# Windowed attention and top-1 experts on one core: the masks move from queries to keys

## What is computed

```python
q = (x @ wq.T + bq).reshape(B, S, H, D)
k = (x @ wk.T + bk).reshape(B, S, H, D)
v = (x @ wv.T + bv).reshape(B, S, H, D)
...
loc = jnp.einsum('bnihd,bnjhd->bnihj', qw, kw) * scale
...
attn = jax.nn.softmax(scores, axis=-1)
out = jnp.einsum('bihj,bjhd->bihd', attn, v).reshape(B, S, HID)
return out @ wo.T + bo
```

## Time and profile before

| | |
|---|---|
| time, median of 3 runs | 444.32 us (442.57 to 446.08) |
| profiled execution | span 442.8 us; no other time of its own is shown |
| instructions | 14658 |
| busy | PE 92%, PEld 77%, DVE 74%, ACT 57%, POOL 50% |
| attention steps | from 37.6 us (scores of window 1) to 312 us (last transposes of attn) |

### The profile page before, as it was taken

One profiled execution on the slowest core, in us unless ns is written; L12 is line 12 of the kernel. 1 busy time (PEld: TensorE's weight loads), 2 busy tenths in 40 slices (PEclk: granted clock), 3 DMA queues, 4 the chain that ended last, 5 costly groups with the idle time before them and its releaser, 6 DMA issues.

```text
span 442.8 us, 14658 instructions
## 1 busy us (share of the span) xinstructions
PE 405.3 (92%) x5747; PEld 339.8 (77%) x5747; DVE 326.1 (74%) x796; ACT 250.6 (57%) x523; POOL 220.4 (50%) x301
## 2 busy tenths in 40 slices
PE   5899799999999999999999899988798998999991
PEld 4758678888888888888888778756577887777891
DVE  6785687758757757757759888563668998899785
ACT  3424665675575575575576576676663555544421
POOL 4361343464464464464464566435733485477540
PEclk9999999999999999999999999999989999999997
DMA  8663740000000000000020000000000011011004
GB/s 240 186 199 111 240 137 4 27 25 0 24 24 0 24 24 0 24 24 0 24 72 4 25 2 3 3 1 2 0 2 2 1 49 47 0 47 49 34 15 143
DMA packets 21720, 20.34 MB, mean 46 GB/s; under 512 B 3133, under 2 KB 21682, under 8 KB 21682
## 3 DMA queue, kind: packets, MB, share of 16 engines
q1 hardware_dynamic: 16900, 15.07, 10.9%
q10 hardware_dynamic: 4782, 4.75, 3.3%
HBM read 15.41 MB, written 4.41 MB: 45 GB/s over the span
## 4 chain that ended last, share of the span: by engine, by line
PE 52%; DVE 26%; ACT 9%; issue 8%; DMA 3%; ACTq 1%; DVEq 0%; POOL 0%; POOLq 0%
DVE row_max_t L1154 10%; PE ps L1461 7%; PE ps L1737 7%; PE ps L1424 7%; PE ps L1562 5%; PE ps L1384 5%; PE ps L1415 4%; PE ps L1438 3%; PE ps L1444 3%; ACT probs L847 3%; DVE k_part L1013 2%; ACT boundsT_t L858 2%; PE ps L1406 2%; DMA rows<-in_L_attn_x_dram 2%; ACT k_part L713 2%
## 5 line engine op out<-in xcount | busy, mean ns | idle before, releaser
L847 ACT ACTIVATE probs<-ps 128x1024 f32<-128x1024 f32 x64 | 62.1, 1022 | 68.2 <-PE ps L1428 68.2
L1154 DVE TENSOR_REDUCE row_max_t<-ps 128x16 f32<-128x2048 f32 x31 | 70.9, 2287 | 3.7 <-PE ps L1415 3.6
L1737 PE MATMUL ps<-w_part,hm_part 128*128 128x256 f32 x384 | 53.8, 289 | 1.8 <-DVE hm_part L1332 1.8
L1415 PE MATMUL ps<-k_part,q_part 32*128 32x128 f32 x1584 | 51.5, 274 | 3.1 <-issue 1.5
L1415 PEld LDWEIGHTS ps<-k_part,q_part 32*128 32x128 f32 x1584 | 46.9, 186 | 9.2 <-issue 7.0
L1562 PE MATMUL ps<-xh_parts,w_part 128*128 128x512 f32 x192 | 53.8, 416 | 0.0
L557 POOL TENSOR_TENSOR q_part<-qf,q_part 128x512 fp32r<-128x512 f32 x32 | 41.0, 1281 | 25.7 <-ACT q_part L695 25.7
L599 POOL TENSOR_TENSOR attn_t<-num_t,rden_t 128x256 f32<-128x256 f32 x32 | 20.0, 624 | 64.7 <-DVE rden_t L1185 64.7
L1737 PEld LDWEIGHTS ps<-w_part,hm_part 128*128 128x128 f32 x384 | 48.2, 190 | 4.8 <-DVE hm_part L1332 2.4
L788 ACT ACTIVATE ffn_rows<-ps,b1s 128x512 f32<-128x512 f32 x32 | 22.0, 687 | 42.2 <-PE ps L1562 34.1
L1562 PEld LDWEIGHTS ps<-xh_parts,w_part 128*128 128x128 f32 x192 | 34.7, 194 | 6.5 <-issue 0.6
(11 more groups left out here) (234 smaller groups left out, 906.4 us busy)
## 6 DMA issues: line engine op xcount, KB each, us to landing
table<-rest_sums SPq DMA_DIRECT2D x4, 1088.0 KB, 6.1
xs<-in_L_attn_x_dram SPq DMA_DIRECT2D x16, 256.0 KB, 2.8
rows<-in_L_attn_x_dram ACTq DMA_DIRECT2D x4, 1024.0 KB, 8.1
out_dram<-yout SPq DMA_DIRECT2D x6, 512.0 KB, 2.9
w<-in_L_ffn_W_dram SPq DMA_DIRECT2D x2, 256.0 KB, 7.6
w<-in_L_ffn_W_dram SPq DMA_DIRECT2D x1, 512.0 KB, 4.2
out_dram<-yout SPq DMA_DIRECT2D x2, 256.0 KB, 2.6
out_dram<-yout ACTq DMA_DIRECT2D x2, 256.0 KB, 2.8
```

What stands on the lines that cost most here:

```text
L847: act.activation(probs[:, 2 * h:2 * h + 2, :], ps[:, 2 * h:2 * h + 2, :], ACT.Exp).then_inc(probs_ready, 1)
L1154: dve.tensor_reduce(row_max[:], ps_all, op=ALU.max, axis=AX.X).then_inc(max_ready, 1)
L1415: last = mm(ps[:, u, (2 * c + a) * P:(2 * c + a + 1) * P], q_part[x][quad(u), s, c, a, :], k_part[y][quad(u), s, c, :], start=(i == 0), st ...
L1737: mm(y, hm_part[a][:, 1 - p, f, c * P:(c + 1) * P], w2_part[b][:, f, :], start=(f == 0 and i == 0), stop=False)
```

## The change

1. The mask and the scale move to the key for the scores: `k_masked` holds, for the two windows of a pair, each key twice (one or the other half), in two parts. The query is kept whole (`q_whole`, high and low part). `scores` multiplies the whole query (stationary) with both masked keys (256 columns): 24 matmuls in place of 48. The turned scores keep masked queries and whole keys.
2. Who masks: the keys DVE (`mask_keys`, four instructions of 512 elements in odd steps, between the reciprocal and the residual), the queries' high part ACT (two of 512 in odd steps, ahead of the exponentials), the queries' low part POOL (one of 512 in each step, where `q_low` stood). ACT makes the whole query's high part in even steps ahead of the exponentials, DVE its low part with two instructions in place of four.
3. Odd steps: DVE's maximum comes first, the keys' low part behind the bounds and guards; on PE the first window's value product goes from ahead of the turned scores to behind the bounds' transpose, and the output product from behind the turned sums to ahead of the turned scores.
4. `k_masked` shares memory with the first expert rows' parts; so their high part is taken in step 31 and no longer in step 30. `w1` shares memory with `ysum` and is loaded at step 24 in place of the start; `split_first_layer` begins a step later.
5. The first pair's keys are masked by ACT (high) and POOL (low) ahead of the steps.

The core of the diff:

```diff
+        k_masked = [xh_parts[:, 0, i].rearrange("p c n -> p (c n)").rearrange("p (w c a n) -> p w c a n", w=2, c=KC, a=2)
+                    for i in range(2)]
...
-        qf = sb("qf", [P, 2, KC, 2, P])
+        q_whole = [sb(f"q_whole{i}", [P, SLOTS, KC, P], fp32r) for i in range(2)]
...
-            def q_low(w, s):
-                need(pool, turned_scores_in_psum, w - 3)
-                pool.wait_ge(q_high_ready, w // 2 + 1)
-                pool.tensor_tensor(q_part[1][:, s], qf[:, s % 2], q_part[0][:, s].bitcast(fp32), ALU.subtract).then_inc(q_ready, 1)
+            def mask_queries_low(w, s, a):
+
+                need(pool, turned_scores_in_psum, w - 2)
+                pool.wait_ge(q_ready, w // 2 + 1)
...
+            def mask_queries_high(w, s):
+
                 need(act, turned_scores_in_psum, w - 2)
-                act.wait_ge(qf_ready, w // 2 + 1)
-                copy(q_part[0][:, s:s + 2], qf[:]).then_inc(q_high_ready, 1)
+                act.wait_ge(q_high_ready, w // 2 + 1)
+                for a in range(2):
+                    last = act.activation(q_part[0][:, s:s + 2, :, a, :], q_whole[0][:, s:s + 2].bitcast(fp32), ACT.Copy,
+                                          scale=q_scale[:, a, 0:1])
+                last.then_inc(q_high_masked, 1)
...
-            def queries_of(w):
-
-                need(dve, q_ready, w)
-                dve.wait_ge(q_in_psum, w // 2 + 1)
-                for k in range(2):
-                    for c in range(KC):
-                        last = dve.scalar_tensor_tensor(qf[:, k, c, :, :],
-                                                        ps_xq[:, (2 * c + k) * P:(2 * c + k + 1) * P].unsqueeze(1).broadcast_to([P, 2, P]),
-                                                        bq_col[:, c:c + 1], q_scale[:], ALU.add, ALU.mult)
-                last.then_inc(qf_ready, 1)
+            def queries_of(w, s):
+
+                dve.wait_ge(q_high_ready, w // 2 + 1)
+                for c in range(KC):
+                    last = dve.scalar_tensor_tensor(q_whole[1][:, s:s + 2, c, :], ps_xq[:, c * 2 * P:(c + 1) * 2 * P].rearrange("p (w n) -> p w n", w=2),
+                                                    bq_col[:, c:c + 1], q_whole[0][:, s:s + 2, c, :].bitcast(fp32), ALU.add, ALU.subtract)
+                last.then_inc(q_ready, 1)
...
+            def mask_keys(w, s):
+
+                need(dve, scores_in_psum, w)
+                dve.wait_ge(k_ready, w // 2 + 1)
+                for i in range(2):
+                    for a in range(2):
+                        dve.tensor_scalar(k_masked[i][:, :, :, a, :], k_part[i][:, s:s + 2].bitcast(fp32), q_scale[:, a, 0:1], None,
+                                          ALU.mult).then_inc(k_masked_ready, 1)
...
             def scores(s):
 
                 for c in range(KC):
+                    for i, (x, y) in enumerate(SPLIT):
+                        for u in range(UNITS):
+                            last = mm(ps[:, u, 2 * c * P:(2 * c + 2) * P], q_whole[x][quad(u), s, c, :],
+                                      k_masked[y][quad(u), s % 2, c, :, :].rearrange("p a n -> p (a n)"),
+                                      start=(i == 0), stop=(i == 2), tile_position=(32 * u, 0))
+                return last
...
-                if not steady and t == NW - 2:
+                if not steady and t == NW - 1:
                     for pair in range(2):
                         take_high(0, 0, pair)
```

More of the change, by code:

```diff
@@ L180, in windowed_attention_then_top1_experts @@
         rest = sb("rest_t", [P, 2, NV])
+        qgf = rest[:].rearrange("p b n -> p (b n)")[:, 0:2 * HID].rearrange("p (c a n) -> p c a n", c=KC, a=2)
         num = sb("num_t", [P, 2, NV])
@@ L580, in step @@
                                        e_val[:, p, :].unsqueeze(2).broadcast_to([P, HEADS, VA]), ALU.mult).then_inc(rest_ready, 1)
-                if live(t + 1, steady) and (steady or t > 0):
-                    q_low(t + 1, (s + 1) % SLOTS)
+                if live(t + 1, steady) and p:
+                    mask_queries_low(t + 1, (s + 1) % SLOTS, 0)
+                if cur and p == 0 and (steady or t > 0):
+                    mask_queries_low(t, s, 1)
                 if cur:
@@ L628, in _ @@
                 w_low(i)
-            q_low(0, 0)
-            q_low(1, 1)
+            pool.wait_ge(dve_const, 4)
+            pool.wait_ge(k_ready, 1)
+            for a in range(2):
+                pool.tensor_tensor(k_masked[1][:, :, :, a, :], k_part[1][:, 0:2].bitcast(fp32),
+                                   q_scale[:, a, :].unsqueeze(1).unsqueeze(1).broadcast_to([P, 2, KC, P]), ALU.mult).then_inc(k_masked_ready, 1)
+            for a in range(2):
+                mask_queries_low(0, 0, a)
             pool.wait_ge(g_bound, 1)
@@ L751, in _ @@
             act.wait_ge(qgf_ready, 1)
-            copy(q_part[0][:, GSLOT], qf[:, 0]).then_inc(qg_high_ready, 1)
+            copy(q_part[0][:, GSLOT], qgf).then_inc(qg_high_ready, 1)
             wide_weight(WV)
@@ L755, in _ @@
             weight_high(WV)
+            queries_of(0, 0)
             keys_of(0, 0)
-            queries_of(0, 0)
+            act.wait_ge(dve_const, 4)
+            act.wait_ge(k_high_ready, 1)
+            for a in range(2):
+                act.activation(k_masked[0][:, :, :, a, :], k_part[0][:, 0:2].bitcast(fp32), ACT.Copy,
+                               scale=q_scale[:, a, 0:1]).then_inc(k_masked_ready, 1)
             load_rows(2)
@@ L820, in step @@
                     copy(aT[:].rearrange("p c n -> p (c n)"), ps_rao[:, 0:HID]).then_inc(aT_ready, 1)
-                if live(t + 1, steady) and p:
-                    queries_of(t + 1, (s + 1) % SLOTS)
                 if not steady and t == 0:
@@ L842, in step @@
                     keep_onehot(0, 0)
+                if ahead and p == 0:
+                    queries_of(t + AHEAD, (s + AHEAD) % SLOTS)
+                if live(t + 1, steady) and p:
+                    mask_queries_high(t + 1, (s + 1) % SLOTS)
                 if prev:
@@ L1144, in step @@
                     low_of_x(t + AHEAD)
-                if live(t + 1, steady) and p:
-                    keys_of(t + 1, (s + 1) % SLOTS)
                 if older:
@@ L1175, in step @@
                 if ahead and p == 0:
-                    queries_of(t + AHEAD)
+                    queries_of(t + AHEAD, (s + AHEAD) % SLOTS)
+                if live(t + 1, steady) and p:
+                    keys_of(t + 1, (s + 1) % SLOTS)
                 early(2)
@@ L1187, in step @@
                 early(5)
+                if live(t + 1, steady) and p:
+                    mask_keys(t + 1, (s + 1) % SLOTS)
                 if not steady and t == 0:
@@ L1411, in scores, with scores_of_globals @@
                 for c in range(KC):
+                    for i, (x, y) in enumerate(SPLIT):
[4 more added lines that the diff above has]
+                return last
+            def scores_of_globals():
+                s = GSLOT
+                for c in range(KC):
                     for a in range(2):
@@ L1602, in step @@
                     queries_of(t + AHEAD)
-                if live(t + 1, steady) and p:
-                    values_of(t + 1)
                 if live(t + 3, steady) and p:
                     turn_x(t + 3)
+                if old and p:
+                    output_product(t - 3)
                 if not steady and t == NW - 2:
-                    pe.wait_ge(qf_ready, NW // 2)
+                    pe.wait_ge(q_ready, NW // 2)
                     pe.wait_ge(v_ready, NW // 2)
@@ L1635, in step @@
                     turn_sums().then_inc(sums_in_psum, 1)
-                if old:
+                if old and not p:
                     output_product(t - 3)
@@ L1703, in _ @@
             pe.wait_ge(kg_ready, 1)
-            scores(GSLOT).then_inc(gs_in_psum, 1)
+            scores_of_globals().then_inc(gs_in_psum, 1)
             turn_x(2)
```

46 lines of the change are left out of this document (31 added, 15 removed).

## The result

The changed kernel takes 477.75 us (median of 4 runs, 475.68 to 481.03), the kernel before 444.69 (442.57 to 446.08, 4 runs): a ratio of 1.076 with an interval of 1.070 to 1.081. The forecast was 457 with a range of 441 to 463. The direction was right, but the loss is 33 us in place of 13, and the time lies outside of the range. The profiled executions have spans of 442.8 and 479.2 us; that of the changed kernel is the slowest of its four (481.03 us), so differences read from the two profiles come out some 3 us larger than those of the medians.

The account below looks back on a forecast made before the run. PE (TensorE), busy 92%, bounds the kernel. Odd steps with masks +21.7 us, even steps and step 31 -9.6, end +0.9: together +13.0 on 444.3, so 457 us, range 441 to 463.

Parts of the forecast that it names:

- Scores: Scores on PE: 24 matmuls of 256 columns take 1.0 us, saving 0.6 us in each step; even steps 7.89 us.
- Masks and turn-taking: Odd steps: DVE masks alternate with GpSimd, PE idles 1.6 us before attn's transposes, step 1.55 us longer; chance 0.52.
- no turn-taking: Rival: masks run at double rate while GpSimd works; odd step +0.4 us, 441 us in all; chance 0.14.
- single rate: Rival: a per-partition scalar takes masks out of double mode; odd step +1.2 us, 452 us in all; chance 0.13.
- The clock has nothing to give back: PE's granted clock shows a nine in all slices but two, so no clock term was priced.
- more than forecast: Rival: late DVE in odd steps also delays the even step's query product and maximum; 464 us; chance 0.10.
- The start: Before the steps: scores(0) waits for DVE's scaled global scores anyway; w1's load moved out gives 0 to -0.5 us.
- they fit into the 2.05 us in which ACT waits: Even step: two activations added before ScalarE's exponentials fit into its 2.05 us wait for the turned scores.
- The end: First expert rows' high part moves from step 30 into 31, ahead of the routing: +0.9 us, between 0 and 1.7.

Follow-up runs that it names:

- experiment 1: Changed kernel, with PE computing the second window's value product three times in odd steps from 3 on, where it would be idle: 468.6 us.
- experiment 2: Changed kernel, with the four DVE masks writing 16 of each window's 128 keys (64 elements in place of 512): 451.3 us.
- experiment 4: Changed kernel, with GpSimd waiting after attn until all four masked keys are written, before making biased and rows: 460.1 us.
- experiment 7: Changed kernel, in step 31 alone the output product back behind the turned sums and the first expert rows' high part behind the maximum: 473.4 us.
- experiment 3: Changed kernel, with each DVE mask writing half of the keys (256 elements in place of 512): 457.9 us.
- experiment 5: Kernel before, with four unused masked keys of 512 elements on DVE between reciprocal and residual in odd steps 3 to 27: 494.4 us.
- Experiment 6: Changed kernel, with ACT's high part of the whole queries in step 0 behind the global scores' exponentials and the copy of x_rest: 473.9 us.
- experiment 8: Changed kernel, ACT masking keys' high part, DVE the low part before the sum, first value product before the bounds' transpose, start as in Experiment 6: 439.3 us.

## Why the forecast was off

Stretch by stretch, from the profiled spans (442.8 and 479.2; the starts of the scores in the two timelines mark the stretches):

| stretch | forecast | measured |
|---|---|---|
| start to step 5 | +0.35 (start 0, steps 2 to 4) | +6.1 (73.30 to 79.36) |
| steps 5 to 24, PE's own time and gaps | +9.5 (10 x (1.55 - 0.6)) | +10.7 (177.08 in experiment 1 less 166.37) |
| steps 5 to 24, clock | 0 | +6.6 (183.70 less 177.08) |
| steps 25 to 30 | +2.85 | +7.1 (57.59 less 50.46) |
| from the last scores on | +0.3 | +5.9 |
| sum | +13.0 | +36.4 (33.1 in the medians) |

**Scores.** Right: 0.98 us for the 24 matmuls (1.0 forecast), and even steps at full clock of 7.91 to 7.97 (7.89).

**Masks and turn-taking.** Right. Mean 752 ns (0.6 to 0.9), alone 0.47, residual at r + 3.30 (3.37), gap 1.58 (1.6), odd step 9.6 (9.5). The rivals "no turn-taking" and "single rate" fall with experiments 2 and 4. The Trainium skill ("SBUF — State Buffer", section "Who interferes with whom") says that whichever of the two issues first has the shared ports for its whole instruction, and that the other is blocked; the rows of experiment 2 agree: the blocked masks end with attn and with biased.

**"The clock has nothing to give back".** This is the step that failed. I read the nines of PEclk as a fact about the kernel, but they were a fact about a PE that was never idle for long: in the steps that I read the longest wait was 0.35 us. My own sum put 1.6 us of idle time into 14 steps and then priced the even steps behind them at full clock, 7.89. The runs show 9.4 to 9.5 in seven of 13. The lower clock is the larger part of the 23.4 us that the forecast missed in the profile, some 17 us: 6.6 in steps 5 to 24, 2.6 in steps 26 and 28, 4.1 at the start (step 5 at 79.36 against 75.22) and 3.4 in the stretch of experiment 7 (27.68 less 24.23). That is an estimate from differences between single executions. With PE filled (experiment 1) or the gap halved (3 and 4) all steps from 5 to 24 are at full clock; the same masks in the old kernel (5) bring the falls there. It was none of the rivals, and the rival "more than forecast" put its price on DVE's lateness, which PE did not feel.

**The start, "0".** Wrong by some 6 us in the profile: 2 for the wait (step 5 at 75.22 in experiment 1 against 73.30 before) and 4 for the clock behind it. I weighed the load of w1 and the scaled scores, not ACT's order: the ACT activations for the queries went ahead of all exponentials, step 0 included, where PE waits for what ACT makes behind them. I had written that they fit into the 2.05 us in which ACT waits; that was read in step 18 and is not so in step 0, where ACT also waits for PE to make the queries. Experiment 6 gives 3.8 us back in the medians.

**The end, "+0.9, between 0 and 1.7".** Mis-sized: +5.9. The moved copies do delay the routing by 0.89 us, as forecast; the pulled output product adds a wait of 1.28 us, because in step 31 ACT is late with aT; and behind both the clock falls (0.91 over the stretch; 1.00 in experiment 7). Experiment 7 gives 5.7 us of it back in the profile, 4.3 in the medians.

**Steps 25 to 30.** Some 2.6 of the 4.3 us missed are two falls (in experiment 1 the steps 26 and 28 are 1.4 and 1.2 shorter). The rest is in the odd steps 25 and 27, which last 11.2 and 10.6 us in the changed kernel: their masks take 2.93 and 3.33 us for four, and small instructions for the layer norm's factors stand between them and the sum; PE's wait for the residual is 1.96 and 2.35 us there. In step 25 PE also waits 1.28 us for the maximum, against 0.54 before. No run isolates either.

The amounts that experiments 1, 6 and 7 give back (9.1, 3.8 and 4.3 us in the medians) can't be added up: the first holds a start without a fall, which is also in the second, and each is a difference of few executions that vary by 5 us in the changed kernel (475.68 to 481.03).

## What to carry to other kernels

An idle gap on TensorE has two prices: its own length, and what the clock does behind it; a row of full clock in the profile of a kernel without gaps says nothing about the version with them. Before work is put on VectorE, look at what GpSimd does in the same microseconds: in double rate the two go one after the other, so place such work where GpSimd is idle (experiment 8) or make GpSimd wait if nobody needs it soon (experiment 4). And a placement that is free in the steady loop has to be priced again in the first and last steps, where other waits count.

## What the runs showed of the hardware

- In the changed kernel a gap of 1.57 to 1.61 us, in odd steps in which PE waits for the sum 0.59 us as well, was followed by 3.4 us at 1.2 GHz in 5 of 11 even steps (4 to 24), and the gaps of 1.96 and 2.35 us behind them both were. The same loop in experiments 6 and 7 gave 5 and 4 of 11, and again both. Gaps of 0.70 and 0.75 us (experiments 3 and 4) were followed by a fall in none of the ten even steps from 6 to 24, gaps of 2.3 us (experiment 5) in 8 of 10. Single ones go either way: 1.58 us in experiment 2 and 1.44 in experiment 3 without a fall, 1.83 in experiment 3 with one.
- The same code needn't behave the same each time: at the start of experiments 1 and 2 PE waited 2.8 us for x_rest as in the changed kernel, without a fall, and the scores of window 1 came at 39.47 and 39.50 in place of 41.69. What decides between one gap and the next wasn't tested.
- A fall of 3.4 us costs about 1.5 us of work here (9.47 less 7.93 for an even step), so a gap of 1.6 us can cost twice its length.
- A VectorE instruction of 64 elements took 170 ns free and 774 ns beside GpSimd. The blocked masks took 677 and 774 ns for 64 elements, 716 and 823 for 256, and 831 to 950 for 512: an eighth of the size did not save much of the blocked time. Two of four were blocked at the smaller sizes, three at 512. Whether fewer instructions for the same elements would cost less wasn't tested.
